# Layer 1 of a two-layer transformer: softmax probabilities transposed by 32x32 blocks and SBUF transfers instead of by the tensor engine

## The reference

```python
b, n, H, HD = 1, 1024, 32, 128
q = rmsnorm((x @ Wq + bq).reshape(b, n, H, HD), gq)
k = rmsnorm((x @ Wk + bk).reshape(b, n, H, HD), gk)
v = (x @ Wv + bv).reshape(b, n, H, HD)
scores = einsum('bhnd,bhmd->bhnm', q, k) / sqrt(HD)
out = einsum('bhnm,bmhd->bnhd', softmax(scores), v).reshape(b, n, H * HD)
return out @ Wo + bo
```

## Time and profile before

| | |
|---|---|
| median of 3 runs | 3272.53 us |
| span of the profiled execution | 3270.4 us (its own time isn't recorded; the median lies 2.1 us above the span) |
| PE, DVE, ACT, POOL busy over the span | 97%, 62%, 42%, 30% |
| layer 1's attention | first exponential at 1296.6 us, last output tile added at 3000.7 us |
| granted TensorE clock | 0.99 of full speed as the mean, 1.00 in 1500 to 2812 us |

### The profile page before, as it was taken

The page is one execution under the profiler, slowest core; times in us unless marked ns, Lnnn a source line. Parts: engine busy times, 40 slices in busy tenths (PEclk is TensorE's granted clock), DMA queues, the critical chain, the costliest instruction groups (busy, mean ns, idle before and its releaser), DMA issues. The chain is left out here.

```text
span 3270.4 us, 58692 instructions
## 1 busy us (share of the span) xinstructions
PE 3188.5 (97%) x19936; PEld 2909.5 (89%) x19936; DVE 2034.0 (62%) x3413; ACT 1389.1 (42%) x2375; POOL 971.0 (30%) x819
## 2 busy tenths in 40 slices
PE   8999999999999978999999999999999999997998
PEld 8989999998999857999999999999999999996786
DVE  3444444444444457777777777777777777777555
ACT  3333333333333322555555555555555555553221
POOL 3333333333333332222222222222222222211765
PEclk9999999999999989999999999999999999999999
DMA  3111111111111001000000000000000000002551
GB/s 115 40 44 40 35 45 41 37 39 45 40 35 45 29 23 34 31 17 31 15 30 15 30 15 30 15 30 15 30 15 30 20 26 29 16 7 78 158 140 55
DMA packets 102601, 128.50 MB, mean 39 GB/s; under 512 B 7297, under 2 KB 66705, under 8 KB 102417
## 3 DMA queue, kind: packets, MB, share of 16 engines
q1 hardware_dynamic: 101696, 126.96, 12.5%
q10 hardware_dynamic: 816, 0.79, 0.1%
q0 software_dynamic: 32, 0.02, 0.0%
HBM read 125.63 MB, written 2.10 MB: 39 GB/s over the span
## 5 line engine op out<-in xcount | busy, mean ns | idle before, releaser
L1287 ACT ACTIVATE b_prob<-b_s_ps,b_shift,b_rstd 128x1024 f32<-128x1024 f32 x252 | 304.2, 1207 | 580.7 <-DVE b_shift L1449 580.7
L1447 DVE TENSOR_REDUCE b_row_max<-b_s_ps 128x1 f32<-128x1024 f32 x252 | 307.2, 1219 | 78.6 <-PE b_s_ps L84 78.5
L82 PE MATMUL b_pj_kq<-b_w_hi,xT_hi 128*128 128x384 f32 x1008 | 341.6, 339 | 1.2 <-DVE b_nat L1417 1.2
L84 PE MATMUL b_pj_kq<-b_w_hi,xT_lo 128*128 128x384 f32 x1008 | 342.1, 339 | 0.0
L83 PE MATMUL b_pj_kq<-b_w_lo,xT_hi 128*128 128x384 f32 x1008 | 341.5, 339 | 0.0
L488 ACT ACTIVATE a_sig<-a_pj 128x512 f32<-128x512 f32 x192 | 114.9, 598 | 498.3 <-PE a_pj L84 498.3
L82 PE MATMUL a_pj<-b_w_hi,xT_hi 128*128 128x256 f32 x1024 | 300.0, 293 | 11.2 <-DVE xT_lo L639 11.1
L84 PE MATMUL a_pj<-b_w_hi,xT_lo 128*128 128x256 f32 x1024 | 290.4, 284 | 0.0
L83 PE MATMUL a_pj<-b_w_lo,xT_hi 128*128 128x256 f32 x1024 | 288.8, 282 | 0.0
L1219 POOL TENSOR_TENSOR b_rstd<-b_mean_sq,power 128x4 f32<-128x4 f32 x128 | 128.9, 1007 | 528.3 <-DVE b_mean_sq L1427 525.0
L1373 PE MATMUL b_t_ps<-ident,b_prob 128*128 128x128 f32 x2048 | 265.6, 273 | 4.8 <-ACT b_prob L1287 4.5
(11 more groups left out here) (273 smaller groups left out, 9126.6 us busy)
## 6 DMA issues: line engine op xcount, KB each, us to landing
b_w_raw<-in_w SPq DMA_DIRECT2D x32, 768.0 KB, 4.3
b_w_raw<-in_w SPq DMA_DIRECT2D x95, 256.0 KB, 3.1
a_w_raw<-in_w SPq DMA_DIRECT2D x32, 256.0 KB, 2.7
a_ow_raw<-in_ow SPq DMA_DIRECT2D x32, 256.0 KB, 3.0
b_ow_raw<-in_ow SPq DMA_DIRECT2D x32, 256.0 KB, 4.5
m_raw_w<-in_mlp_w SPq DMA_DIRECT2D x28, 256.0 KB, 3.0
m_raw_z<-in_mlp_z SPq DMA_DIRECT2D x28, 256.0 KB, 3.8
m_raw_s<-in_mlp_s SPq DMA_DIRECT2D x28, 256.0 KB, 4.9
```

The lines of the kernel that those rows point to most:

```text
L82: pe.matmul(out, w_hi, x_hi, start=first, stop=False)
L84: return pe.matmul(out, w_lo, x_hi, start=False, stop=last)
L1287: act.activation(prob[:, :], score_banks(h, t)[:, :], ACT.Exp, bias=shift[:, t:t + 1], scale=rstd[b][:, t, 1:2], accum_out=row_sum[:, t:t ...
L1447: dve.tensor_reduce(row_max[:, t:t + 1], score_banks(h, t)[:, :], AX_X, ALU.max).then_inc(max_done, 1)
```

## The change

The probabilities `prob` (128 queries x 1024 keys, now two buffers) are no longer transposed on PE. DVE transposes their 32x32 blocks in place of the copy (`transpose_blocks`, into the new `blocks`), and for each pair of query tiles SP issues 16 SBUF-to-SBUF transfers (`move`) that bring the 4x4 grid of block groups into transposed order: each takes 32 partitions x 8 x 64 numbers, in runs of 256 bytes, into `pT_lo`. ACT copies the high part from there (`prob_hi`, half a batch at a time), and POOL instead of DVE subtracts it in place (`prob_lo`). The queries of a transposed batch stand in the order (group, tile, query in group), which `out_hi` and `out_lo` undo. The two banks of `t_ps` become a second score buffer. `values` moves from slots 3.. to slots 5.., `output_tile` from 5.. to 7.., with a `split_part` one slot ahead of the values; `v_batch` is two slots later, and weights are split in slots 1, 2 and 4. The query's inverse RMS is multiplied into q together with k (`scale_kq`, 512 instead of 256 numbers per partition), so that `maxima` is one instruction, and it now always stands behind the transpose on DVE.

```diff
-        prob = sb("prob", [P, TOK])
-        row_max = sb("row_max", [P, NT])
+        prob = [sb(f"prob{i}", [P, TOK]) for i in range(2)]
+        blocks = [sb(f"blocks{i}", [P, TOK // BLK, BATCH, BLK]) for i in range(2)]
...
-        s_ps = bank("s_ps", [P, TOK])
-        t_ps = bank("t_ps", [P, TOK])
+        s_ps = [bank(f"s_ps{i}", [P, TOK]) for i in range(2)]
...
         def quarter(h, b, cur, rest, s):
-            n = (s - 3) % 8
-            if s >= 3:
+            n = (s - 5) % 8
+            if s >= 5:
                 return (h, b, n // 2, n % 2) if cur else None
             return (h - 1, 1 - b, n // 2, n % 2) if rest else None
+        def split_part(h, cur, rest, s):
+            n = (s - 4) % 8
+            if s >= 4:
+                return (h, n // 2, n % 2) if cur else None
+            return (h - 1, n // 2, n % 2) if rest else None
...
+        SPLITS = {1: 0, 2: 1, 4: 2}
...
+            def move(h, i):
+                sp.wait_ge(blocked, NT * h + BATCH * (i + 1))
+                to = f(pT_lo[i % 2][:, :, :])
+                for a in range(GROUPS):
+                    of = blocks[i % 2][:, a::GROUPS, :, :].rearrange("p m u q -> p m (u q)")
+                    for g in range(GROUPS):
+                        sp.dma_start(to[a * BLK:(a + 1) * BLK, :, g * BATCH * BLK:(g + 1) * BATCH * BLK],
+                                     of[g * BLK:(g + 1) * BLK, :, :]).then_inc(moved[i % 2], 16)
+            def step(h, b, cur, rest, nxt, more):
+                if cur and more:
+                    aw.load(sp, w, h + 2)
+                    load_bias(h + 2, b)
+                if rest:
+                    move(h - 1, NB - 1)
+                if cur:
+                    move(h, 0)
+                if nxt:
+                    load_output_weights(h + 1)
+                if cur:
+                    move(h, 1)
+                    move(h, 2)
...
+            def prob_lo(h, i, part):
+                pool.wait_ge(pT_hi_done, 2 * NB * h + 2 * i + part + 1)
+                cut = slice(part * NT // 2, (part + 1) * NT // 2)
+                pool.tensor_tensor(pT_lo[i % 2][:, cut, :], f(pT_lo[i % 2][:, cut, :]), f(pT_hi[i % 2][:, cut, :]),
+                                   ALU.subtract).then_inc(pT_lo_done, 1)
...
+            def prob_hi(h, i, part):
+                act.wait_ge(moved[i % 2], MOVED * (2 * h + i // 2 + 1))
                 wait(act, pv, NB * h + i - 1)
+                cut = slice(part * NT // 2, (part + 1) * NT // 2)
+                act.activation(pT_hi[i % 2][:, cut, :], f(pT_lo[i % 2][:, cut, :]), ACT.Copy).then_inc(pT_hi_done, 1)
...
-            def transpose_probs(h, t):
-                pe.wait_ge(exp_done, NT * h + t + 1)
-                wait(pe, pT_lo_done, NT * h + t)
-                for m in range(NT):
-                    cut = slice(m * P, (m + 1) * P)
-                    last = pe.transpose(t_ps[:, cut], prob[:, cut], sh.ident[:, :])
-                last.then_inc(p_tr, 1)
...
+            def scale_kq(g, bg, i):
+                dve.wait_ge(rstd_ready, NB * g + i + 1)
+                both = nat[i][:, :, 0:2 * HD].rearrange("p t (k d) -> p t k d", k=2)
+                dve.tensor_tensor(both, both, rstd[bg][:, BATCH * i:BATCH * (i + 1), :].unsqueeze(3).broadcast_to(
+                    [P, BATCH, 2, HD]), ALU.mult).then_inc(kq_scaled, 1)
...
-                dve.tensor_reduce(row_max[:, t:t + 1], score_banks(h, t)[:, :], AX_X, ALU.max).then_inc(max_done, 1)
-                dve.wait_ge(max_done, NT * h + t + 1)
-                dve.tensor_scalar(shift[:, t:t + 1], row_max[:, t:t + 1], rstd[b][:, t, 1:2], -1.0,
-                                  ALU.mult, ALU.mult).then_inc(shift_done, 1)
+                dve.tensor_reduce(shift[:, t:t + 1], s_ps[t % 2][:, :], AX_X, ALU.max, negate=True).then_inc(shift_done, 1)
+            def transpose_blocks(h, t):
+                i, u = t // BATCH, t % BATCH
+                dve.wait_ge(exp_done, NT * h + t + 1)
+                if u == 0:
+                    wait(dve, moved[i % 2], MOVED * (2 * h + i // 2))
+                dve.transpose(blocks[i % 2][:, :, u, :], prob[t % 2][:, :]).then_inc(blocked, 1)
```

More of the change, by code:

```diff
@@ L1100, in l1_attention @@
         y_ps = bank("y_ps", [P, HALF])
-        ln_banks = [s_ps[:, 0:HALF], s_ps[:, HALF:], t_ps[:, 0:HALF], t_ps[:, HALF:]]
+        ln_banks = [s[:, j * HALF:(j + 1) * HALF] for s in s_ps for j in range(2)]
         w_lo_done, proj = aw.lo_done, aw.proj
@@ L1204, in _ @@
             sp.dma_start(bo_sb[:, :], bo.partition_broadcast(P)).then_inc(const_in, 16)
[L1205 to L1209, removed]
+            steps(sp, step)
             sp.wait_ge(pv, NB * HEADS - 1)
@@ L1234, in step @@
                         v_low(*v_batch(h, b, cur, nxt, s))
+                    if split_part(h, cur, rest, s):
+                        prob_lo(*split_part(h, cur, rest, s))
                     if cur and s == 3:
@@ L1240, in step @@
                                            ALU.subtract).then_inc(ow_lo_done, 1)
-                    if nxt and more and s in (0, 2, 4):
-                        aw.split_low(pool, h + 2, b, s // 2)
+                    if nxt and more and s in SPLITS:
+                        aw.split_low(pool, h + 2, b, SPLITS[s])
             steps(pool, step)
@@ L1302, in step @@
                         kq_high(h + 1, 1 - b, s // 2)
[L1303 to L1306, removed]
+                    if split_part(h, cur, rest, s):
+                        prob_hi(*split_part(h, cur, rest, s))
                     if cur:
@@ L1312, in step @@
                         act.activation(ow_hi[b][:, :], ow_raw[:, :], ACT.Copy).then_inc(ow_hi_done, 1)
-                    if nxt and more and s in (0, 2, 4):
-                        aw.split_high(act, h + 2, b, s // 2)
+                    if nxt and more and s in SPLITS:
+                        aw.split_high(act, h + 2, b, SPLITS[s])
             steps(act, step)
@@ L1344, in values @@
             def values(h, b, i, part):
+                pe.wait_ge(pT_lo_done, 2 * NB * h + 2 * i + part + 1)
                 if part == 0:
[L1347 removed]
                     pe.wait_ge(v_lo_done, NB * (h + 1))
@@ L1358, in scores @@
                     pe.wait_ge(kq_lo_done, NB * (h + 1))
-                wait(pe, exp_done, NT * h + (t - 1 if peeled(h, HEADS - 1) and t else t))
+                wait(pe, exp_done, NT * h + t - 1)
                 cut = slice(t * P, (t + 1) * P)
@@ L1499, in step @@
                     if nxt and s % 2 == 0:
-                        scale_k(h + 1, 1 - b, s // 2)
+                        scale_kq(h + 1, 1 - b, s // 2)
                     if q and q[3]:
@@ L1504, in step @@
                         kq_low(h + 1, 1 - b, s // 2)
-                    early = s % 2 and not peeled(h, HEADS - 1)
-                    if early:
-                        for t in scored_in(h, cur, s):
-                            maxima(h, b, t)
                     if rest and s == 0:
-                        prob_lo(h - 1, NT - 1)
+                        transpose_blocks(h - 1, NT - 1)
                     if cur and s:
-                        prob_lo(h, s - 1)
-                    if not early:
-                        for t in scored_in(h, cur, s):
-                            maxima(h, b, t)
+                        transpose_blocks(h, s - 1)
+                    for t in scored_in(h, cur, s):
+                        maxima(h, b, t)
                     if output(h, b, cur, rest, s):
```

68 lines of the change are left out of this document (26 added, 42 removed).

## The result

The changed kernel takes 3451.18 us (median of 4 runs, 3444.91 to 3454.34), the kernel before 3272.82 on the same chip: 1.054 times as long, 95% interval 1.0526 to 1.0556. The profiled execution's span is 3446.7 us, 176.3 more than before.

What follows compares the result with a forecast made beforehand. PE bound the kernel before at 53.7 us per head; after, a DVE-ACT-POOL loop of 53.3 plus 6.6 of collisions makes 59.9, +198 us with head 0 and the drain, so 3470 us, range 3250 to 3560.

Steps and rivals of the forecast that it cites:

- The total: Whole kernel: span of 3468 us, with the difference between span and median 3470 us.
- the forecast of slower: Whole kernel: slower than before by more than 0.2% (6.5 us), chance 0.74.
- What PE gives up: PE in layer 1: 64 probability transposes per head, 6.4 us, leaving PE alone 47.3 us per head.
- Rival C: Layer 1: PE stays the bound, so the kernel gets faster, 3082 us; chance 0.06.
- The loop through DVE, ACT and POOL: Layer 1, odd maximum to odd maximum without PE: 12.79 us per pair, 53.3 us per head with weight splits.
- the exponential: ACT's term in the DVE, ACT and POOL loop: 1.20 us from start to what follows.
- The transfers: SP's moves: 0.475 us an issue, 9.7 us a move, 12.65 per pair, hidden under 12.79; at 0.59 13.6, binding.
- The collision: Even slots: `scale_kq` sits out POOL's `prob_lo`, 2.2 us more each, three per head, 6.6 us, 59.9 per head.
- rival B: Even slots: transfers land 0.6 to 1.1 us later, no collision, loop near 53.3, 3268 us; chance 0.20.
- Rival D: Moves: slower by transfers, 256-byte runs at twice 27 ns 3535 us, or 0.7 us an issue 3425; chance 0.17.
- The drain: Kernel's end, from the last exponential: 21.9 us where before it was 12.2.
- A reading of the rows before: DVE in the kernel before: waits long in a slot only for PE, 0.67 us ahead of the odd maximum.

Runs made afterwards that it cites:

- e10: Changed kernel with both DVE transposes early (even one behind `means`), POOL's `prob_lo` behind the scaling, PE's k/q transposes and scores before odd-slot values: 3096.8 us, 0.9467.
- e9: e5 with PE doing k and q transposes and scores ahead of the first half of the values in odd slots: 3241.6 us, 0.9908.
- e6: e5 with each move as one transfer of all 128 partitions instead of 16, blocks misplaced: 3292.7 us, 1.0063.
- e12: e5 with each move as 8 transfers of 64 partitions instead of 16 of 32, blocks misplaced: 3295.2 us, 1.0069.
- e5: Changed kernel with POOL's `prob_lo` in even slots waiting until DVE has scaled k and q: 3408.7 us, 1.0413.
- e4: Changed kernel with each move as 8 transfers of 64 partitions instead of 16 of 32, blocks misplaced: 3476.1 us, 1.0618.
- e2: Changed kernel with the even slot's DVE transpose first of all, plus an added DVE wait for earlier values: 3517.8 us, 1.0750.
- e3: Changed kernel with DVE's transposes early in both even and odd slots, plus the added DVE wait for earlier values: 3514.4 us, 1.0738.
- e7: e3 with e5's edit, POOL's `prob_lo` in even slots behind the scaling: 3447.3 us, 1.0535.

## Why the prediction was right, and where not

The total was right within 19 us and the forecast of slower was right; the reason was half right, and the closeness of the total is luck.

- **What PE gives up**: 6.4 us a head, to 47.3. Right; e10 runs at 47.1. Rival C's 3082 us is what the change could be worth, and e10's order gets 3097 of it.
- **The loop through DVE, ACT and POOL**: 12.79 us per pair and 53.3 a head with the splits. The mechanism was right, the size 0.41 a pair too large: 12.38 and 51.8 in e9. Half of that is the exponential, 1.11 us to what follows it and not 1.20, twice a pair. So this loop by itself leaves 1.9 of the 6.4 us that PE gives up, not 0.4. The forecast also said that no instruction of PE is in it. In e6 and e12, at 53.8, PE was: the transposes of k and q stood behind the values, and the values behind `prob_lo`. That 53.8 lies near 53.3 is two errors that cancel, 1.5 too many and 2.0 left out.
- **The transfers**: the step that failed. It took 0.475 us an issue from loads to other tiles, over the 0.59 that it kept for the range. Measured 0.65, landing 2.1: a move of 12.0 us and not 9.7. In the prediction's own formula that is (12.0 + 15.6) / 2 = 13.8 per pair, 55.2 a head; e5 has 57.3. PE's lower clock after its waits, up to 1.7 us a head by the estimate above, is most of the rest.
- **The collision**: the mechanism and its size were right (2.87 us, behind a `prob_lo` at the end of the inverse RMS), the number wrong: 0.58 a head instead of three. It failed through the issue rate too: at 0.65 the blocks land after the scaling, as rival B had it for 0.52 to 0.55. Where they land early (e4: 3.7 a head) the kernel runs at 59.9 a head, the forecast's 59.9.
- So a head of the changed kernel, by the differences of the runs, is 51.8 for the loop (e9), 2.0 for k and q behind the values (e12 less e9), 3.5 for the transfers (e5 less e12) and 1.1 for collisions, against a forecast of 53.3 + 6.6. The middle two were measured with POOL's new order, which itself puts `prob_lo` later, so their split in the changed kernel isn't shown. The transfers and three collisions a head, delays that exclude each other, cost nearly the same, and the number came out by that.
- **Rival D**, at 0.7 us an issue 3425: the right mechanism and the nearest account, though its own formula gives (13.1 + 15.6) / 2 = 14.35 a pair, 57.4 a head and 3395 us. Its other price, 256-byte runs at twice 27 ns, is refuted. In the transfer view of 1500 to 2812 us (queue: packets, MB, share of 16 engines):

```profile
q1 hardware_dynamic: 401197, 122.78, 47.6%
```

  0.476 x 16 x 1312 / 401197 = 24.9 ns a packet, and 98% are under 512 bytes (392493 of them; the moves' runs have 256). The Trainium skill ("DMA: Bandwidth & Descriptors", Specifications) expects a read-modify-write below 512 bytes; no run here shows a cost of it beyond the 27 ns that the forecast had for a run of 512 bytes.
- **The drain**: forecast 21.9 us, measured 33.0. It missed that the last transpose waits behind `out_lo`, 5.8 us, and at 0.65 an issue the last move is 2.3 longer. The other 3 lie behind POOL's last subtraction: from 3167.07 us 7.05 to the last output, where the forecast had 3.9. PE's clock was low there again (0.50 from 3164.8 to 3169.4), and an output tile stands ahead of the last half of the values.
- **A reading of the rows before**: it says that DVE waits long only for PE, 0.67 us. Rows 7 have it wait 1.63 for ACT's `q_hi`. The sum doesn't use it, but this is the wait in which the late values showed.

## What to carry to other kernels

When a change shortens the bound engine, follow the dependent chain through the in-order programs of all the others before asking how busy they are: here the next loop was 1.9 us a head below the old bound (forecast 0.4), and the order of PE's own work took even that. Price a transfer by its issues, and find what is queued behind its consumer on each engine; with k and q ahead of the values on PE, 16 issues a move left at most 0.2 us a head above the loop (51.8 and 51.6 in e9). Of several fixes for one chain each may look worthless or harmful alone (e2, e3, e7), because removing one delay, or the wait that it needs, makes another appear; try them with the order of the queues that they run into.

## What was unexpected of the hardware

- An issue from SBUF to SBUF cost SP 0.61 us with 256 runs and 32 partitions, 0.65 with 512 runs and 64, and 0.465 with one transfer of all 128 partitions (e6), which landed 4.6 us later where the small ones took 2.1. Twice the runs cost 6% more.
- DVE's scaling with both inputs in SBUF, started 0.06 us behind a POOL subtraction of 2.39, took 2.87 instead of 0.69, nearly the whole of POOL's instruction; e2 shows it in 87 scalings of 87. The maximum, which reads PSUM, kept its 1.19 when it started inside a `prob_lo` (2018.88, with POOL busy from 2017.98).
- One idle stretch of PE of 2.87 us was followed by a granted clock of 0.53 for the next 3.4 us. One of 1.60 us (before 2003.80) was followed by 1.00 in 2004 to 2008.
